# Layer norms and routing in the lead, weighing in pieces of two slots: an attention and expert block on one core

## The reference, cut to what matters

```python
xn = layernorm(x)
# attention, 8 heads of 16, each with two maps of 8 features
scores = einsum('bqhif,bkhif->ibhqk', q, k) * 8 ** -0.5
att = softmax(scores)[0] - diff_weight * softmax(scores)[1]
o = einsum('bhqk,bkhe->bqhe', att, v)
a = ((o * rms(o) * norm_w) @ Wo.T + bo) * (1 - diff_weight)
# experts: one shared, eight routed, each token to its best two
vals, idx = top_k(sigmoid(xn @ Wg), 2); vals /= vals.sum()
f = (ffn_shared(xn) + sum of vals * ffn_expert(xn)) / 3   # ffn: silu(x W1) * (x W3) @ W2, 256 wide
out = x + a + f
```

## Time and profile before

| | us |
|---|---|
| three timed runs, median (lowest, highest) | 683.73 (679.42, 683.97) |
| the profiled execution, as timed | 677.72 |
| its span in the profile | 675.9 |
| its mean granted TensorE clock | 0.956 of full |

### The profile page before, as it was taken

The page is one execution under the profiler, slowest core; times in us unless marked ns, Lnnn a source line. Parts: engine busy times, 40 slices in busy tenths (PEclk is TensorE's granted clock), DMA queues, the critical chain, the costliest instruction groups (busy, mean ns, idle before and its releaser), DMA issues.

```text
span 675.9 us, 11161 instructions
## 1 busy us (share of the span) xinstructions
PE 620.1 (92%) x3570; PEld 326.6 (48%) x3570; DVE 478.9 (71%) x1025; ACT 401.4 (59%) x782; POOL 243.6 (36%) x328
## 2 busy tenths in 40 slices
PE   6698989999999999999999989999999989999894
PEld 5244444455454544555455445545545545545321
DVE  5788868788777877677666666667667666777274
ACT  3004655656566656666667656666666656666772
POOL 7304450257667740232233322223323223323211
PEclk8556989999999999999999999999999999999997
DMA  3717459121313123152433315142241422210292
GB/s 105 203 55 135 48 97 146 13 75 41 104 40 112 48 92 96 46 168 71 116 93 101 106 46 156 61 143 79 76 134 58 137 76 81 83 46 13 68 254 66
DMA packets 54754, 62.26 MB, mean 92 GB/s; under 512 B 7048, under 2 KB 38792, under 8 KB 54696
## 3 DMA queue, kind: packets, MB, share of 16 engines
q1 hardware_dynamic: 49832, 51.68, 29.7%
q0 software_dynamic: 4544, 9.35, 4.3%
q10 hardware_dynamic: 320, 0.52, 0.3%
HBM read 27.50 MB, written 16.59 MB: 65 GB/s over the span
## 4 chain that ended last, share of the span: by engine, by line
PE 70%; DVE 16%; issue 7%; ACT 3%; DMA 1%; POOL 1%; SPq 1%; DVEq 0%; ACTq 0%
PE F L1059 16%; PE O L1025 14%; PE ST L1011 13%; PE F L1071 9%; PE S L992 6%; DVE rowmax L750 6%; DVE hid L781 4%; DVE ub L772 3%; PE F L926 2%; PE F L931 1%; PE F L922 1%; PE F L963 1%; PE ST L992 1%; PE F L1043 1%; PE F L979 1%
## 5 line engine op out<-in xcount | busy, mean ns | idle before, releaser
L750 DVE TENSOR_REDUCE rowmax<-S 128x1 f32<-128x512 f32 x490 | 323.7, 682 | 157.6 <-PE S L992 156.9
L586 ACT ACTIVATE probs<-ST 128x512 f32<-128x512 f32 x490 | 265.8, 595 | 81.7 <-PE ST L1011 77.9
L992 PE MATMUL S<-kop,qop 62*128 62x512 f32 x490 | 196.6, 475 | 8.2 <-DMA kop<-kparts 3.5
L1011 PE MATMUL ST<-qop,kop 64*128 64x512 f32 x490 | 181.8, 450 | 8.3 <-ACT probs L586 5.2
L1025 PE MATMUL O<-probs,vop 128*32 128x512 f32 x1024 | 148.2, 612 | 0.1
L421 POOL DMA_INDIRECT yt<-ysb,xst x78 | 76.6, 982 | 120.8 <-DMA yt<-ysb,xst 106.6
L1011 PEld LDWEIGHTS ST<-qop,kop 64*128 64x128 f32 x490 | 74.0, 187 | 79.0 <-issue 37.3
L992 PEld LDWEIGHTS S<-kop,qop 62*128 62x128 f32 x490 | 80.7, 191 | 26.5 <-DVE rowmax L750 21.4
L380 POOL TENSOR_SCALAR o_inv<-o_inv,ndw 128x8 f32<-128x8 f32 x32 | 10.2, 319 | 201.5 <-DVE o_inv L796 201.3
L1059 PE MATMUL F<-xsT,wrt_all 128*128 128x256 f32 x312 | 76.6, 388 | 2.2 <-ACT xsT L567 1.2
L410 POOL DMA_INDIRECT xs<-xn,slot_i x64 | 62.1, 971 | 25.3 <-DVE rowmax L750 16.0
(11 more groups left out here) (141 smaller groups left out, 559.9 us busy)
## 6 DMA issues: line engine op xcount, KB each, us to landing
wrt_all<-in_wexp SPq DMA_DIRECT2D x39, 384.0 KB, 3.1
qop<-qparts SPq DMA_DIRECT2D x64, 128.0 KB
kop<-kparts SPq DMA_DIRECT2D x60, 128.0 KB
xs<-xst SPq DMA_DIRECT2D x13, 387.0 KB, 10.8
xst<-xs SPq DMA_DIRECT2D x39, 129.0 KB, 2.9
base<-in_x SPq DMA_DIRECT2D x8, 256.0 KB, 4.1
xn<-yt SPq DMA_DIRECT2D x8, 256.0 KB, 5.0
out_x<-base SPq DMA_DIRECT2D x8, 256.0 KB, 2.7
```

The lines of the kernel that those rows point to most:

```text
L586: A(probs[:, n % NP, :], st_bank(n)[:, :], ACT.Exp, scale=SCALE).then_inc(s_p, 1)
L750: V.reduce_max(rowmax[hf][:, 1 - k % 2, q // 2 % HC, (2 * q + k // 2) % QT:(2 * q + k // 2) % QT + 1], s_bank(n)[:, :], AX).then_inc(s_mx, 1)
L992: mm(s_bank(n)[:, :], qop[b % 2][at:at + TERMS, c, t * P:(t + 1) * P], kop[b % 2][at:at + TERMS, c, :], start=True, stop=True, tile_positi ...
L1011: mm(st_bank(n)[:, :], kop[b % 2][at:at + BAND, c, t * P:(t + 1) * P], qop[b % 2][at:at + BAND, c, :], start=True, stop=True, tile_positio ...
```

## The change

1. *Lead.* x of all batches is loaded at the start, the statistics of batches 2 to 7 are taken by VectorE ahead of the first row maximum, with one ln_pow and one ln_bias for batches 2 to 7. q and k of batch 1 and v of batch 0 are computed before the first score. ScalarE normalises all batches (slots -11 to -6), transposes and gate logits follow two and three slots later, GpSimd adds the bias rows in slots -9 to -2. The constants (`bo_row`, `woT` and others) are computed on GpSimd. The memsets of `qop[1]` and `kop[1]`, for which SP waits, come behind ln_pow of batches 2 to 7.
2. *Routing* on VectorE in slots 0 to 8, the prefix sum in slot 4, GpSimd's steps in 4 and 5, scatters from slot 8, two or three a slot. Seven of the 13 fills go into the lead (slots -10 to -3), six into slots 1 to 6.
3. *Tiles* in every second slot: shared ones in 6 to 36, routed ones in 38 to 114. up(j, 0) at k = 3 of the even slot, up(j, 1) at k = 1 of the odd one, gate_u ahead of the odd slot's row maxima, tanh behind the even slot's exponentials, down(j) and the next tile's do_xsT at k = 3 of the odd slot.
4. *Weighing* of two slots in one piece at k = 1 of even slots, with 12 buffers `probs`. Other batch pieces at k = 3 in even slots, k = 1 in odd ones. squares, add_proj, residues and max_parts stand at k = 1 of even slots, beside the weighing.
5. *Smaller.* Residues of q and k (b of 1 and more) are taken from an SBUF copy that ScalarE makes, not from the bank. tanh, gate_u and gate_hid work in place in `hid`. m rows go by two DMAs instead of four. The projection uses `F[1]`. Batch 7 is combined in slot 128.

The diff, cut to its core:

```diff
-    VW, NP = 32, 8
+    VW, NP = 32, 12
-    POST = 6
+    POST = 7
-    SH_AT = [10 + 2 * i for i in range(SH_TILES)]
-    RT_AT = [43 + 71 * r // (RT_TILES - 1) for r in range(RT_TILES)]
-    TILE_AT = SH_AT + RT_AT
+    RT_AT = [38 + 2 * r for r in range(RT_TILES)]
+    SH_AT = [at for at in range(6, SLOTS, 2) if at not in RT_AT][:SH_TILES]
+    TILE_AT = sorted(SH_AT + RT_AT)
-    COMBINE_AT = [LOAD_Y0 + 2 + b for b in range(BATCH - 1)]
-    LN_AT = [None, None, 0, 1, 3, 4, 6, 7]
-    PREFIX_AT = 14
-    SCAT0 = 18
+    COMBINE_AT = [LOAD_Y0 + 2 + b for b in range(BATCH)]
+    NORM_AT = [None, None] + [x - 13 for x in range(2, BATCH)]
+    PREFIX_AT = 4
+    SCAT0 = 8
+    FILL_AT = [-10, -9, -8, -6, -5, -4, -3, 1, 2, 3, 4, 5, 6]
+    def rest(slot):
+        return 3 if slot >= 0 and slot % 2 == 0 else 1
+        R_DVE = {n: n for n in range(19)} | {24: 22, 25: 23, 34: 28, 35: 29, 36: 30, 37: 31, 38: 32, 39: 33, 40: 34}
+        R_POOL = {n: 4 if n < 24 else 5 for n in (19, 20, 21, 22, 23, 26, 27, 28, 29, 30, 31, 32, 33)}
...
 GpSimd
-            ln_pow(1)
+            ln_pow(1, 2)
...
-            G.memset(qop[1][:, :, :].bitcast(f32), 0.0).then_inc(s_pads, 1)
-            G.memset(kop[1][:, :, :].bitcast(f32), 0.0).then_inc(s_pads, 1)
...
+            constants()
+            ln_pow(2, BATCH)
+            G.memset(qop[1][:, :, :].bitcast(f32), 0.0).then_inc(s_pads, 1)
+            G.memset(kop[1][:, :, :].bitcast(f32), 0.0).then_inc(s_pads, 1)
...
 ScalarE
+                A(qparts[:, 0, :], bank[:, :], ACT.Copy).then_inc(s_q1, 1)
+                if b >= 1:
+                    A(qparts[:, 1, :].bitcast(f32), bank[:, :], ACT.Copy).then_inc(s_qf, 1)
...
-                    act.wait_ge(s_av, slot - 1)
+                    act.wait_ge(s_av, slot - 2)
...
 VectorE
+            ln_stats(2)
             residue_q(0)
             residue_k(0)
+            for b in range(3, BATCH):
+                ln_stats(b)
+            ln_bias(3, 2, BATCH)
...
 TensorE
+            do_q(1)
+            do_k(1)
+            do_v(0)
...
                     if k == 1:
-                        if 1 <= slot <= SLOTS:
+                        if 2 <= slot <= SLOTS and slot % 2 == 0:
+                            weigh(slot - 2)
                             weigh(slot - 1)
-                        other(slot)
...
+                    j = tile_at(slot)
+                    if j is not None and k == 3:
+                        up(j, 0)
+                    j = tile_at(slot - 1)
+                    if j is not None and k == 1:
+                        up(j, 1)
+                    if k == rest(slot):
...
+                        other(slot)
+                    if k == 3:
+                        r = routed(tile_at(slot + 1))
                         if r is not None:
                             do_xsT(r)
-                    if k == 3:
                         j = tile_at(slot - 1)
                         if j is not None:
                             down(j)
-                        j = tile_at(slot)
-                        if j is not None:
-                            up(j, 0)
-                            up(j, 1)
```

More of the change, by code:

```diff
@@ L290, in _ @@
             sp.dma_start(wqkvT[:, :, :], wqkv).then_inc(s_wqkv, 16)
-            load_x(1)
+            for b in range(1, 4):
+                load_x(b)
             sp.dma_start(wg[:, :], wgate).then_inc(s_small, 16)
@@ L296, in _ @@
             sp.dma_start(woT[:, :], wo).then_inc(s_small, 16)
+            for b in range(4, BATCH):
+                load_x(b)
             sp.dma_start(wsh[:, :], wexp[E]).then_inc(s_wsh, 16)
-            load_x(2)
             sp.wait_ge(s_pads, 2)
@@ L356, in _, with ln_pow, constants @@
             gp.wait_ge(s_half, 1)
[L358 to L365, removed]
+            def ln_pow(b0, b1):
+                gp.wait_ge(s_ln, LN_A * b1)
+                at = slice(QT * b0, QT * b1)
+                G.tensor_tensor(rstd[:, at], ve[:, at], half[:, 0:1].to_broadcast([P, QT * (b1 - b0)]), ALU.pow).then_inc(s_rstd, 1)
+            def constants():
+                gp.wait_ge(s_small, 16 * 5)
+                G.tensor_scalar(omd[:, :], dw_col[:, :], -1.0, 1.0, ALU.mult, ALU.add).then_inc(s_const, 1)
+                G.tensor_scalar(ndw[:, :], dw_col[:, :], -1.0, None, ALU.mult).then_inc(s_const, 1)
+                gp.wait_ge(s_const, 2)
+                G.tensor_tensor(wos[:, :], nw_col[:, :], omd[:, :], ALU.mult).then_inc(s_const, 1)
+                G.tensor_scalar(bo_row[:, :], bo_row[:, :], omd[:, 0:1], None, ALU.mult).then_inc(s_const, 1)
+                gp.wait_ge(s_const, 4)
+                G.tensor_scalar(woT[:, :], woT[:, :], wos[:, 0:1], None, ALU.mult).then_inc(s_wo, 1)
             def add_bias(b):
-                if b == 0:
-                    gp.wait_ge(s_const, 4)
                 gp.wait_ge(s_xn, QT * (b + 1))
@@ L475, in _ @@
                 b, s = slot // QUADS, slot % QUADS
-                x = norm_at(slot)
-                if x is not None:
-                    ln_pow(x)
-                    normalise(x)
+                x = slot + LEAD - 2
+                if 0 <= x < BATCH:
                     add_bias(x)
@@ L490, in _ @@
                 if slot >= SCAT0:
-                    for i in range(3):
+                    for i in range(2 + slot % 2):
                         if scat < TOPK * NT:
@@ L813, in add_proj @@
                 dve.wait_ge(s_ysh, 2 * (b + 1))
-                if last:
+                if b == BATCH - 1:
                     dve.wait_ge(s_cmb, 8 * (b + 1))
@@ L858, in _ @@
                     add_shared(j, i)
-                x = norm_at(slot)
-                if x is not None:
-                    ln_stats(x)
+                j = tile_at(slot - 1)
+                if j is not None:
+                    gate_u(j)
                 for k in range(4):
@@ L878, in _ @@
-                    if k == 2:
+                    at = slot + LEAD - (1 if slot >= 0 else 0)
+                    n = at // 8 - 1
+                    if at % 8 == 0 and 0 <= n < 2 * BATCH and k == (1 if slot >= 0 else 0):
+                        for i in range(3):
+                            max_parts(n, i)
+                    if k == 1:
+                        if s == 4 and 1 <= b < BATCH:
+                            squares(b - 1)
+                        if s == 8 and 1 <= b < BATCH:
+                            add_proj(b - 1)
+                        if s == 10 and 1 <= b + 2 < BATCH:
+                            residue_q(b + 2)
+                        if s == 12 and 1 <= b + 2 < BATCH:
+                            residue_k(b + 2)
```

224 lines of the change are left out of this document (104 added, 120 removed).

## The result

The kernel after takes 644.22 us (median of 4 runs, 642.34 to 644.69), the kernel before beside it 682.55 (4 runs). The ratio is 0.9439, with a 95% interval of 0.9398 to 0.9480: 38 us faster, where 16 were forecast. The profiled execution has a span of 640.5 us against 675.9.

What follows compares the result with a forecast made beforehand. TensorE, busy 92%, was taken as the bound, losing 0.66 us per tile, mainly behind VectorE's row maxima and gate steps. +9 - 21.4 - 2.7 - 1 = -16 us; from the timed median 683.7 that gave 667.5, range 649 to 690.

Steps and rivals of the forecast that it cites:

- Part 3: First to last expert tile, tiles in every second slot: 505.9 us against 508.6, so 2.7 saved.
- Part 1: Lead before slot 0: first row maximum near 28, slot 0 starts at 64 instead of 55.0, +9 us.
- Part 2: Slots 0 to 6, up to the first up-projection, bound by VectorE: 33 us instead of 54.4, 21.4 saved.
- 0.40 lost per tile: Tile stretch: mean loss 0.19, ScalarE's second copies 0.07 and unexplained 0.14, over 54 tiles; bounds 0.2 and 0.87.
- work 484.3: First to last tile: TensorE work in us without losses, from the earlier trace's prices for slots, tiles and batches.
- lost otherwise: Routed tiles of the kernel before: 0.14 us of the 0.55 lost per tile left unexplained, carried into the forecast.
- the hand schedule: Two-slot tile period worked out: a bare pair loses 0.85 us; with batch pieces the mean is 0.19.
- these and the other small edits: Part 3: added waits, residues and m rows with half the DMAs, 12 probability buffers, tanh in place, costed at nothing.
- Part 4: Tail after the last tile: ScalarE's exponentials still set 2.3 to 2.4 us per slot; -1 us, bounds -4 and +2.
- Slower: Rival at the odd slot: batch pieces don't fill the hole, each tile loses 1.02, 33 us more, 701; chance 0.13.
- No change: Rival: half clock and fills start slot 0 at 72, tiles lose 0.55 as now, 683.7 us; chance 0.17.
- More: Rival: fixed-price ln_pow, transposes raise the clock, slot 0 at 58, loss 0.22 per tile, -32 us, 651.7; chance 0.15.

Runs made afterwards that it cites:

- the last experiment: Kernel after with no fills ahead of the first m rows, single weighings up to slot 6, late gate only in slots 1, 3, 5 of a batch: 654.85 us, ratio 0.9471.
- tokens_apart: Kernel after with the transposes of a tile's tokens one piece earlier in the odd slot, no longer beside the down-projection: 664.37 us, ratio 0.9593.
- the named piece alone: Kernel before with only the weighing in pieces of two slots, 12 buffers for probabilities, and tanh and gate operations in place: 724.04 us, ratio 1.0575.

## Why the prediction was wrong

Point by point, in the order of its parts. The direction was right and the size less than half of what was measured. The main mechanism was not: 12.4 of the 16 us stood on the lead, which the runs show to be worth nothing, and the gain is in Part 3, which had 2.7.

**Part 1, the lead: right.** First row maximum 25.67 (forecast 28), ln_pow 4.20 (I took 4), slot 0's first score 62.46, released by the m rows' DMA (64); +7.4 for +9. The m rows landed 4.62 us behind the fills (4.00 and 3.35 in the other two traces of this kernel), and those of slot 8 in the last experiment 4.26; with no fills about, in the tail, they took 2.27. The rule of the Trainium skill (DMA: Bandwidth & Descriptors, Queues, rings and completion order) that a ring's descriptors are consumed in order agrees with this. By the forecast it gave 64 to 66, and without it 61.5; the start lies between. The last experiment had no fills ahead of slot 0's rows and started slot 0 at 61.6, on the row maxima, as the sum had it; so the fills cost about 1 us there.

**Part 2, slots 0 to 6: right in size, wrong in what it means.** First up-projection at 97.93 (forecast 97), 35.5 us for 33: -18.9 for -21.4. For the missing 2 the chain has two candidates: the second and third weighing, 3.46 and 3.57 at the lower clock where the forecast had only the first there, and GpSimd's steps, which were to "just fit" and stand in the chain for 4.0 us. Yet putting the whole lead back costs nothing. Parts 1 and 2 are -11.5 together, and of those 4 x 2.31 = 9.2 are four slots without a tile that went from ahead of the tiles to behind them. That they reappear in Part 3's stretch stands in the forecast; that Parts 1 and 2 are then worth 2 us does not.

**Part 3, first tile to last: the step that failed.** Measured 484.5 us (97.93 to 582.44, the starts of the first and last up-projection) for 505.9 forecast, -24.1 for -2.7. These 21.4 us are more than the 19.4 by which the span was missed (640.5 for 675.9 - 16). The term is the 0.40 lost per tile on top of "work 484.3". The total is no more than that work alone. In a batch the forecast had 16 x 2.31 + 8 x 3.42 + 8.3 = 72.6 and 8 x 0.40 = 3.2 lost, 75.8 in all; 71.95 were measured. The chain of the batch splits them: the 64 pairs of scores take 23.0 us where 64 x 0.33 are 21.1, so 1.9 us are still waits, 0.24 a tile for the 0.40; and the work itself costs about 2.3 less than 72.6. Two things were wrong in the forecast.
- The work was priced by the earlier trace rows, as if a piece had one price. Placed otherwise the same instructions are cheaper: down-projection 0.95 for 1.13, transposes 0.44 for 0.59, weighing 1.85 for 1.98, v 0.89 for 1.1, k 0.86 for 1.06, against 2.12 for 1.92 of the up-projection. Over a batch these are -1.6, -1.0, -1.0, -0.5 (q, k, v and projection) and +1.8. Where the same 448 or 449 weight loads stand in a batch, busy time is 74.2 us in the kernel before with even tiles and 71.95 after, 2.3 a batch. tokens_apart shows the mechanism on one piece.
- Waits of 0.07 for ScalarE's second copies and 0.14 "lost otherwise" were carried over. The list of waits above has 6.8 us for bank `F[2]`, 0.18 for each of 38 tiles, enough for the 0.14; the token copy had 1.2 us. The change removes these waits, and the forecast had costed them as staying. The 0.24 left is near the mean of 0.19 that the hand schedule gave. That it is near is partly luck, for the schedule used the old prices (a piece of 0.59 where 0.44 stand).

I had cost "these and the other small edits" at nothing. Much of the change was there and in the order: moving gate, tokens or pieces back costs 1.9 to 3.2 us of a batch each, all of them with single weighings 6.5.

**Part 4, the tail: right.** 58.1 us after 582.44, 57.8 before: +0.3 for -1.

**The rivals.** *Slower* named the odd slot, and it is there that the split alone, on the kernel before, loses what it wins; in the kernel after the wait has 0.27 left. *No change* fell with the first tile at 97.9. *More*, 651.7, had the right place (a lower loss per tile, 0.22 for 0.24 measured) beside a wrong one (slot 0 at 58) and was still 7 us short, for it too kept the old prices.

## What to carry to other kernels

When an engine is near full, take neither its prices nor its waits from the old order: measure a whole period (here one batch) as a window, split it into idle and busy, and ask for every moved piece which work stands before it, who must copy its result before its reader comes, and which bank it keeps until then. The list of waits of the kernel before, by line, names these banks ahead of any run. Do not judge parts of a reordering one at a time: here the split, the spacing and the early gate each bought next to nothing alone, the named piece alone cost 5.8%, and the split paid only with the small pieces and copies in their new places. A stretch moved from ahead of the main loop to behind it shows as a gain in the windows of its stage and as none in the run.

## What the runs showed of the hardware that was not expected

A TensorE piece has no price of its own. The same eight matmuls of the down-projection took 0.89 to 0.96 us right behind the token transposes and 1.09 to 1.13 behind scores; the same two of k 0.86 beside the up-projection and 1.05 behind the weighing. In the kernel after and in the run with the tokens apart all but the first two or three of these eight matmuls start 0.11 us behind the one before; the difference stands where the piece meets what was before it. That the shape of the tile that the array held just before is the cause fits all of these, but was not tried by itself.

GpSimd's power took 4.20 us over 24 columns and 1.02 over 4: 0.16 a column and 0.38 fixed, by these two.

On the chips where the kernel before took 692 to 694 us the kernel after lost more (656 and 659), and its traces have holes of 3.2 to 4.0 us, some 20 us apart, from 124 to 230 us, while the tokens are scattered. In several of them ScalarE and VectorE stand still together, and the profile ascribes them to nothing in the program. In the kernel after beside the last experiment:

```profile
126.30 3.50 another core or an unknown queue
```

The trace of the kernel after at 640.5 us has none there; what causes them stays open.
